# Counts as logarithms in the graph mask, the second graph weights split inside the first attention, and routing operations in another order

## The reference, cut to what matters

```python
def gat_conv(x, edge_index, W, a_src, a_dst, bias, heads, out_ch, concat):
    xl = (x @ W).reshape(n, heads, out_ch)
    alpha_src = einsum('nhc,hc->nh', xl, a_src)
    alpha_dst = einsum('nhc,hc->nh', xl, a_dst)
    e = leaky_relu(alpha_src[src] + alpha_dst[dst], 0.2)
    m = segment_max(e, dst)
    e = exp(e - m[dst])
    s = segment_sum(e, dst)
    alpha = e / (s[dst] + 1e-16)
    out = segment_sum(xl[src] * alpha[:, :, None], dst)
...
h = gat_conv(x, ..., W1, HEADS=4, concat=True)
h1 = relu(layer_norm(h, g1, be1)) + (x @ Wr1 + br1)
h = layer_norm(gat_conv(h1, ..., W2, heads=1), g2, be2) + (h1 @ Wr2 + br2)
...
gate_logits = h2 @ Wg                      # 625 x 8, the best expert of each token
hid = relu(h2 @ W1[expert] + b1[expert])   # 768 -> 3072
y = hid @ W2[expert] + b2[expert]          # 3072 -> 768
```

## Time and profile before

| | |
|---|---|
| median of 3 runs | 1123.75 us (1120.61 to 1124.71) |
| the profiled execution, its own time | 1123.52 us |
| its span in the profile | 1121.6 us |
| PE busy | 1042.5 us (93% of the span) |
| DVE / ACT / POOL busy | 741.3 / 564.8 / 157.0 us |
| mean granted clock of TensorE | 0.974 of full speed |
| transfers | 155.60 MB, mean 139 GB/s |

### The profile page before, as it was taken

How to read it: one execution, slowest core, us unless ns; L and a number is a source line. 1 busy time by engine, 2 the same in 40 slices (tenths; PEclk the granted TensorE clock), 3 DMA queues, 4 the chain that set the end, 5 groups by cost and what they waited for, 6 DMA issues and landing times.

```text
span 1121.6 us, 19089 instructions
## 1 busy us (share of the span) xinstructions
PE 1042.5 (93%) x6181; PEld 651.5 (58%) x6182; DVE 741.3 (66%) x1334; ACT 564.8 (50%) x754; POOL 157.0 (14%) x175
## 2 busy tenths in 40 slices
PE   5999889997999999989989499999999999999997
PEld 3555557764775775556767345555555555555554
DVE  6667767786547764269976698931119898989511
ACT  2667755530451343168843477721118787777311
POOL 2000000040003531054001201100102020302000
PEclk9999999998999999989999599999999999999999
DMA  8300030004507400030014599950007999999200
GB/s 306 104 0 0 1 113 1 1 1 154 126 1 153 81 6 1 1 109 3 2 61 128 214 388 322 390 214 14 24 0 284 386 362 371 373 363 387 84 17 3
DMA packets 92263, 155.60 MB, mean 139 GB/s; under 512 B 36507, under 2 KB 36587, under 8 KB 92214
## 3 DMA queue, kind: packets, MB, share of 16 engines
q1 hardware_dynamic: 89814, 149.20, 38.5%
q0 software_dynamic: 2400, 5.77, 1.4%
HBM read 153.21 MB, written 7.77 MB: 144 GB/s over the span
## 4 chain that ended last, share of the span: by engine, by line
PE 74%; DVE 13%; issue 5%; DMA 3%; ACT 3%; POOL 1%; DVEq 1%; SPq 0%; ACTq 0%; POOLq 0%
PE psum L1493 31%; PE psum L1742 17%; PE psum L1717 16%; DMA low<-in_L_ffn_W_dram 2%; DVE area L1355 2%; PE psum L1481 2%; PE psum L1531 2%; PE psum L1726 2%; DVE smalls L999 1%; PE psum L1632 1%; DVE area L1326 1%; PE psum L1713 1%; DVE area L1086 1%; ACT area L889 1%; ACT low L896 1%
## 5 line engine op out<-in xcount | busy, mean ns | idle before, releaser
L1493 PE MATMUL psum<-area,low 128*125 128x512 f16 (+4 forms) x1116 | 249.3, 384 | 9.9 <-DVE low L1197 6.0
L1355 DVE TENSOR_TENSOR area<-low,area 128x1536 f16<-128x1536 f32 x144 | 246.0, 1754 | 13.4 <-ACT area L948 13.2
L1717 PE MATMUL psum<-area,low 128*128 128x512 f16 x972 | 220.3, 381 | 0.0
L1742 PE MATMUL psum<-area,low 128*128 128x384 f16 x1296 | 219.3, 328 | 0.0
L948 ACT ACTIVATE area<-low 128x1536 f16<-128x1536 f32 x138 | 200.3, 1484 | 37.6 <-DMA low<-in_L_ffn_W_dram 28.8
L1493 PEld LDWEIGHTS psum<-area,low 128*125 128x125 f16 (+2 forms) x1116 | 144.2, 142 | 105.7 <-issue 59.9
L1493 PE MATMUL psum<-area 125*128 125x64 f16 (+10 forms) x1452 | 195.6, 289 | 9.0 <-DVE area L1326 6.0
L1742 PEld LDWEIGHTS psum<-area,low 128*128 128x128 f16 x1296 | 127.0, 98 | 80.9 <-issue 1.7
L1493 PEld LDWEIGHTS psum<-area 125*128 125x128 f16 (+3 forms) x1452 | 126.8, 122 | 60.8 <-DVE area L1326 12.4
L1717 PEld LDWEIGHTS psum<-area,low 128*128 128x128 f16 x972 | 95.2, 98 | 113.7 <-issue 2.5
L959 ACT ACTIVATE low<-psum 128x512 f32<-128x512 f32 x54 | 31.9, 591 | 158.7 <-PE psum L1717 155.7
(11 more groups left out here) (235 smaller groups left out, 1147.8 us busy)
## 6 DMA issues: line engine op xcount, KB each, us to landing
low<-in_L_ffn_W_dram SPq DMA_DIRECT2D x144, 768.0 KB, 8.2
area<-in_L_gnn_W_dram SPq DMA_DIRECT2D x2, 3072.0 KB, 12.0
area<-in_L_gnn_Wr_dram SPq DMA_DIRECT2D x2, 3072.0 KB, 15.6
low<-in_x_dram SPq DMA_DIRECT2D x10, 336.0 KB
area<-in_L_ffn_Wv_dram SPq DMA_DIRECT2D x6, 384.0 KB, 6.3
area<-in_L_ffn_Wq_dram SPq DMA_DIRECT2D x6, 384.0 KB, 6.9
area<-in_L_ffn_Wk_dram SPq DMA_DIRECT2D x6, 384.0 KB, 6.1
area<-in_L_ffn_Wp_dram SPq DMA_DIRECT2D x2, 1152.0 KB, 6.8
```

Of the source, the lines that this page charges most:

```text
L1355: dve.tensor_tensor(low_, raw_view(u), high_, ALU.subtract).then_inc(low_ok, 1)
L1493: ins = pe.matmul(place(name)[0:parts, at:at + w], left(q), right(q)[:, at:at + w], start=(q == 0), stop=(q == k - 1))
L1717: ins = pe.matmul(psum[:, (c % 2) * BANK:(c % 2 + 1) * BANK], ht[x_][:, k, :], w1_s[c][w_][:, k, :], start=False, stop=(k == KD - 1 and x_ ...
L1742: ins = pe.matmul(psum[:, (4 + q) * BANK:(4 + q) * BANK + D // 2], hidT[c % 2][x_][:, j, :], w2_s[c][w_][:, j, q * D // 2:(q + 1) * D // 2 ...
```

## The change

1. **Counts as logarithms.** POOL raises the counts to at least 1, ACT takes their logarithm in place (`logs`), POOL subtracts it from `absent`. DVE's L1126 so adds the mask and the logarithm at once. ACT's Exp gives the row's sum itself (`accum_out`), DVE only adds 1e-16 to it, and PE turns the matrix straight after Exp.
2. **W2 split inside the first attention.** `graph_high` and `graph_low` of W2 are done in two halves of 3072 columns, ACT's at steps 7 and 11, DVE's one step later. `RES1_HALVES` goes from steps 8, 15, 17, 19 to 8, 13, 15, 18. Wr2 is loaded when the second half is done. Behind the attention, `h1T_low(0)` goes ahead of the last join.
3. **Routing.** `ids_first` comes right behind the number of blocks; the table and `routed` come ahead of the places of the tokens; five pairs of small operations for the places become three larger ones; `tokens_low(0)` goes ahead of DVE's wait for `routed`.

```diff
-RES1_HALVES = {8: (1, 0), 15: (1, 1), 17: (2, 0), 19: (2, 1)}
+SPLIT_AT = (7, 11)
+RES1_HALVES = {8: (1, 0), 13: (1, 1), 15: (2, 0), 18: (2, 1)}
...
@@ SP
-            sp.wait_ge(g_low, 1)
+            sp.wait_ge(g_low, 2)
             sp.dma_start(v3(staged, KH), g_Wr2.rearrange("(k p) n -> p k n", p=128)).then_inc(wr2g_in, 16)
...
@@ POOL, ahead of the norms of the first attention
+            for d in range(T):
+                pool.wait_ge(absent_ok, d + 1)
+                pool.tensor_scalar(counts[:, d, :], counts[:, d, :], 1.0, None, ALU.max).then_inc(clamped, 1)
+            for d in range(T):
+                pool.wait_ge(logs_ok, 1 if d < T - 1 else 2)
+                pool.tensor_tensor(absent[:, d, :], absent[:, d, :], counts[:, d, :], ALU.subtract).then_inc(mask_ok, 1)
...
@@ ACT, behind the counting
+            def logs(d0, d1):
+                act.wait_ge(clamped, d1)
+                act.activation(counts[:, d0:d1, :], counts[:, d0:d1, :], ACT.Ln).then_inc(logs_ok, 1)
+
+            logs(0, T - 1)
             no_edge(T - 1)
+            logs(T - 1, T)
...
@@ ACT, attention
                     if 1 <= i <= n:
                         act.wait_ge(neg_ok, g)
-                        act.activation(zbuf[(g - 1) % 4], zbuf[(g - 1) % 4], ACT.Exp, scale=-1.0,
-                                       bias=negm[:, (g - 1) % 4:(g - 1) % 4 + 1]).then_inc(exp_ok, 1)
+                        q = slice((g - 1) % 4, (g - 1) % 4 + 1)
+                        act.activation(zbuf[(g - 1) % 4], zbuf[(g - 1) % 4], ACT.Exp, scale=-1.0, bias=negm[:, q],
+                                       accum_out=rsum[:, q]).then_inc(exp_ok, 1)
...
+                    if layer == 1 and i in SPLIT_AT:
+                        q = SPLIT_AT.index(i)
+                        graph_high(w2g_in, w2_parts, slice(q * KH * D // 2, (q + 1) * KH * D // 2))
...
@@ DVE, attention
+                        if g < T:
+                            dve.wait_ge(mask_ok, i + 1)
                         dve.tensor_tensor_reduce(z, z, absent[:, i % T, :], 1.0, 3e38, ALU.add, ALU.min,
                                                  negm[:, g % 4:g % 4 + 1]).then_inc(neg_ok, 1)
...
                         dve.wait_ge(exp_ok, g)
-                        dve.tensor_tensor_reduce(z, z, counts[:, t, :], 1.0, 1e-16, ALU.mult, ALU.add,
-                                                 rsum[:, q]).then_inc(prob_ok, 1)
+                        dve.tensor_scalar(rsum[:, q], rsum[:, q], 1e-16, None, ALU.add).then_inc(sum_ok, 1)
...
+                    if layer == 1 and i - 1 in SPLIT_AT:
+                        q = SPLIT_AT.index(i - 1)
+                        graph_low(q + 1, w2_parts, slice(q * KH * D // 2, (q + 1) * KH * D // 2))
...
-            dve.wait_ge(absent_ok, T)
...
@@ DVE, between the attentions
             for t in range(3):
                 residual_row(t)
-            graph_low(1, w2_parts)
             for t in range(3):
                 join_residual(t)
-            for t in range(3, T):
-                residual_row(t)
-                join_residual(t)
-            for t in range(3):
+            residual_row(3)
+            join_residual(3)
+            residual_row(4)
+            h1T_low(0)
+            join_residual(4)
+            for t in (1, 2):
                 h1T_low(t)
-            graph_low(2, wr2_parts)
+            graph_low(3, wr2_parts)
...
@@ DVE, routing: behind nblk
+            done(dve, ("ids0",))
+            emptied_by(("ids0",), dve.tensor_scalar(ids_first, place(("ids0",), 1), float(NOWHERE), None, ALU.add))
+            was_emptied(dve, ("ids0",))
+            dve.sem_inc(ids0_ok, 1)
             link(dve.tensor_scalar(active, nblk, 0.0, None, ALU.is_gt))
...
             dve.tensor_copy(nblocks, nblk_sum[0:1, E - 1:E]).then_inc(routed, 1)
+            dve.sem_inc(hid_relu, 2)
+            link(dve.tensor_scalar(base8, start, float(BR), None, ALU.mult))
+            link(dve.tensor_tensor(cum[:, 0:T, :], cum[:, 0:T, :], spread(base8, (P, T, E), 2), ALU.add))
+            link(dve.tensor_tensor(sel, sel, cum[:, 0:T, :], ALU.mult))
+            link(dve.tensor_reduce(pos_f, sel, AX_X, ALU.add))
...
+            dve.tensor_copy(ids_all[:, 1:NB + 1], ids_f).then_inc(ids_ok, 1)
+            tokens_low(0)
             dve.wait_ge(routed, 1)
-            dve.sem_inc(hid_relu, 2)
...
@@ PE
-                        pe.wait_ge(prob_ok, before_ + i)
+                        pe.wait_ge(exp_ok, before_ + i)
```

More of the change, by code:

```diff
@@ L778, in xl2_copy, with graph_high @@
                 emptied_by(("xl2", t), act.activation(xl2[:, t, :], place(("xl2", t), D, P), ACT.Copy, scale=1.0 / SCALE_UP))
-            def graph_high(loaded, high_low):
+            def graph_high(loaded, high_low, columns=slice(0, KH * D)):
                 act.wait_ge(loaded, 16)
-                act.activation(high_low[0], staged, ACT.Copy, scale=SCALE_UP).then_inc(g_high, 1)
+                act.activation(high_low[0][:, columns], staged[:, columns], ACT.Copy, scale=SCALE_UP).then_inc(g_high, 1)
             def weights_high(loaded, whole, high_low):
@@ L1113, in weights_low, with graph_low @@
                                          op1=ALU.subtract).then_inc(w_low, 1)
+            def graph_low(n, high_low, columns=slice(0, KH * D)):
+                dve.wait_ge(g_high, n)
+                dve.scalar_tensor_tensor(out=high_low[1][:, columns], in0=staged[:, columns], scalar=SCALE_UP,
+                                         in1=high_low[0][:, columns], op0=ALU.mult, op1=ALU.subtract).then_inc(g_low, 1)
             def graph_attention(layer, heads, width, agg, bias_row, behind=None):
@@ L1173, in _ @@
             shifted1(T - 1).then_inc(epi_b, 1)
-            def graph_low(n, high_low):
-                dve.wait_ge(g_high, n)
-                dve.scalar_tensor_tensor(out=high_low[1], in0=staged, scalar=SCALE_UP, in1=high_low[0], op0=ALU.mult,
-                                         op1=ALU.subtract).then_inc(g_low, 1)
             def residual_row(t):
@@ L1370, in _, with tokens_low @@
             was_emptied(dve, ("gate", T - 1))
+            def tokens_low(b):
+                dve.wait_ge(hthi_ok, b + 1)
+                dve.tensor_tensor(ht[1], turned, ht[0], ALU.subtract).then_inc(ht_ok, 1)
             def by_token(ap, n=E):
@@ L1398, in _ @@
             link(dve.tensor_tensor(order, active_sum, active, ALU.subtract))
-            link(dve.tensor_scalar(base8, start, float(BR), None, ALU.mult))
-            done(dve, ("ids0",))
-            ins = dve.tensor_scalar(ids_first, place(("ids0",), 1), float(NOWHERE), None, ALU.add)
-            emptied_by(("ids0",), ins)
-            was_emptied(dve, ("ids0",))
-            dve.sem_inc(ids0_ok, 1)
-            for t in range(T):
-                link(dve.tensor_tensor(cum[:, t, :], cum[:, t, :], base8, ALU.add))
-                link(dve.tensor_tensor_reduce(junk8, cum[:, t, :], sel[:, t, :], 1.0, 0.0, ALU.mult, ALU.add,
-                                              pos_f[:, t:t + 1]))
-            link(dve.tensor_tensor(reached, by_token(pos_f, NB + 1), spread(first_rows, (P, T, NB + 1), 2), ALU.is_ge))
-            link(dve.tensor_reduce(block_of, reached[:, :, 1:NB + 1], AX_X, ALU.add))
-            link(dve.scalar_tensor_tensor(out=row_in, in0=block_of, scalar=float(-BR), in1=pos_f, op0=ALU.mult, op1=ALU.add))
-            for t in range(T):
-                dve.tensor_scalar(row_hot[:, t, :], iota128, row_in[:, t:t + 1], None, ALU.is_equal)
-            link(dve.tensor_tensor(here, reached[:, :, 0:NB], reached[:, :, 1:NB + 1], ALU.subtract))
-            dve.tensor_tensor(here16, here, by_token(token_id, NB), ALU.mult).then_inc(spots_ok, 1)
             def over(ap, keep):
@@ L1422, in _ @@
             link(dve.tensor_tensor(match, match, prod, ALU.mult))
-            done(dve, ("ids",))
-            emptied_by(("ids",), dve.tensor_scalar(ids_f, place(("ids",), NB), float(NOWHERE), None, ALU.add))
-            was_emptied(dve, ("ids",))
-            dve.tensor_copy(ids_all[:, 1:NB + 1], ids_f).then_inc(ids_ok, 1)
             for q, what in enumerate((iota8, order)):
@@ L1436, in _ @@
             dve.tensor_copy(nblocks, nblk_sum[0:1, E - 1:E]).then_inc(routed, 1)
+            dve.sem_inc(hid_relu, 2)
[3 more added lines that the diff above has]
+            link(dve.tensor_reduce(pos_f, sel, AX_X, ALU.add))
+            link(dve.tensor_tensor(reached, by_token(pos_f, NB + 1), spread(first_rows, (P, T, NB + 1), 2), ALU.is_ge))
+            link(dve.tensor_reduce(block_of, reached[:, :, 1:NB + 1], AX_X, ALU.add))
+            link(dve.scalar_tensor_tensor(out=row_in, in0=block_of, scalar=float(-BR), in1=pos_f, op0=ALU.mult, op1=ALU.add))
+            for t in range(T):
+                dve.tensor_scalar(row_hot[:, t, :], iota128, row_in[:, t:t + 1], None, ALU.is_equal)
+            link(dve.tensor_tensor(here, reached[:, :, 0:NB], reached[:, :, 1:NB + 1], ALU.subtract))
```

(12 more changed lines are left out.)

15 lines of the change are left out of this document (7 added, 8 removed).

## The result

The changed kernel takes 1111.99 us (median of 5 runs, 1110.96 to 1117.14); the kernel before, run beside it, 1121.01 us (median of 5). The ratio is 0.992, 95% interval 0.9903 to 0.9937: 9.0 us less, against 9.2 forecast. In a later series, beside 23 runs of the kernel before (1120.91 us), it took 1110.57, a ratio of 0.9898 (0.9878 to 0.9918). The ratios leave disturbed executions out and are not exactly the quotient of the two medians (in the later series that would be 0.9908). So the total came as forecast. The steps did not all: this profile and twelve runs show that two errors in the first attention cancelled each other, and that the routing gained its part in another way.

The account below looks back on a forecast made before the run. PE, busy 93% of the span, was taken as the bound, so only its waits or lower clock could be won. 5.1 between the attentions, 2.7 clock and 1.4 routing made 9.2 us less: about 1114 us, range 1108 to 1119.

Parts of the forecast that it names:

- The start: Start of the first attention: POOL's subtractions and DVE's operations take turns, first agg at 161.3 instead of 157.6, 3.7 us lost.
- rival B: Start of the first attention: POOL does not hold DVE up, first agg 4.6 us earlier, total 1110 us; chance 0.24.
- 3 x 1.5: Start of the first attention: three POOL subtractions of 1.5 us each fall between DVE's first four operations.
- the chain from 139.9 us: Mask preparation from ACT's first free moment: source row copied at 148.8 instead of 148.1, DVE's first pair 150.3 instead of 149.6.
- rival E: Routing and clock give nothing: transfers set the pace, or the start's wait lowers the clock; 1116 us, chance 0.12.
- L1134 taken out: First attention: PE's last four waits for DVE's multiplication by the counts go, 4.8 us gained.
- The splits: W2's halves on ACT and DVE inside the first attention: 1.0 us exposed, bounds 0 and 12 us.
- Rival C: First attention: W2's splits are exposed, 11 us more there, total 1125 us, no difference; chance 0.13.
- The attention's end: PE's end of the first attention: 241.2 + 3.7 - 4.8 + 1.0 = 241.1 us, rounded down to 240.8.
- Between the attentions: From the first attention to xl2(0): start at 264.7 instead of 269.8, 5.1 us; clock holds, another 2.7 us.
- The routing: Routing before the experts: rows 1.24 us earlier, third unit's split 1.35 us earlier; 1.4 us taken, ends 0 and 2.2.
- D: First attention: ACT reloads activation tables with every unit, 42 us slower, total about 1156 us; chance 0.03.

Follow-up runs that it names:

- logarithms alone: Only the counts as logarithms (point 1 of the change) put into the kernel before: 1118.27 us, ratio 0.9965.
- rows first: Changed kernel, but SP holds weight unit 5, with 6 and 7 behind it, until the first block's rows have landed: 1116.68 us, ratio 0.994.
- DVE's masks: Changed kernel, but idle DVE does the last maximum and all five subtractions instead of POOL: 1107.20 us, ratio 0.9859; run again 1104.82 us, ratio 0.9853.
- the split alone: Only the split of W2 inside the first attention (point 2 of the change) put into the kernel before: 1116.86 us, ratio 0.9956.

## Why the prediction was right, and where it was not

- **The start.** The mechanism was right (POOL and DVE work in turns, and rival B is false), its size was too large. The second Exp was to come 5.9 us later, made up of 0.7 for a later first pair, 0.7 for the rest of a subtraction and "3 x 1.5". It came 3.75 us later, counted from the source row's turns, and PE's two waits for Exp came to 3.6 us where 5 or more were named. The first 0.7 is a slip: the terms of the chain from 139.9 us add up to 148.2 and not to 148.8, and DVE had its first pair when it had it before (3.08 us behind the turns, 3.07 before). The second 0.7 was 0.1. The 1.5 us of one subtraction was right (1.52), but three of DVE's operations were stretched by only 1.2 us each. From the source row's turns to the first agg it was 12.55 us instead of 11.01, so 1.5 us were lost and not 3.7. But the step stopped there: the wait that it foresaw took the clock down, which cost another 1.65 us (logarithms alone) to 3.2 us (this trace). I had named this only as a part of rival E; together the start cost 3.2 to 4.7 us. Rival B's price was wrong too: with POOL out of the way the first agg comes 9.01 us behind the turns, a gain of 2.0 us and not 0.9.
- **L1134 taken out.** The forecast was 4.8 us, and 6.06 were measured. The term left out what PE loses after each wait, some 0.3 us apiece.
- **The splits.** The forecast was 1.0 us; 1.1 to 1.2 were measured. The attention takes 92.87 us with them (rows first) and 91.78 without (logarithms alone) at nearly the same lapse, and its part behind the second head's source row takes 76.60 with them (DVE's masks) and 75.38 without. In the trace two waits of 0.45 and 0.16 us stand at steps 7 and 11. Rival C is out. Without the logarithms the splits cost 3.2 us.
- **The attention's end** was forecast for 240.8 and came at 240.76. That is luck: +3.7 - 4.8 + 1.0 = -0.1 stood for about +4.7 - 6.1 + 1.2 = -0.2.
- **Between the attentions.** The forecast was a start of xl2(0) at 264.7 us and 7.8 us for it; measured were 264.80 and 8.01. PE's wait is 1.56 us for 1.5, and row 4's copy and `h1T_low` are last in the chain, as said. This carried the result: 4.57 us of the way from the attention's end to xl2(0), and 2.5 us of clock.
- **The routing.** The forecast was 1.35 us; about 1.2 are shown in the traces, by another way, and that they agree is luck again. The step said that the rows "land, are turned and have their high part 1.24 us earlier". They landed 0.3 us earlier on the mean of three traces each, since the weight transfers ahead set their landing. What remains is the 0.94 us behind `routed` that `tokens_low` no longer waits for. The step had this too, but took 0.7 us of register loads off again, between `tokens_low` and the third split; they do not show there, since L1376 starts 0.88 us after L1394, as L1355 started 0.87 after L1449.
- **Rivals D and E.** There were two table loads of 1.28 us, no more, and both lay under waits (ACT still waits 0.81 us for POOL after the first and 0.99 for DVE after the second), so D is out. The Trainium skill ("ScalarE: Activation LUTs", table sets) names a set that holds both functions; this program, as compiled, loads twice. Of E, the lapse at the start came true, but both the routing and the clock at xl2(0) gave their part.

What the sum did not hold at all is how single executions differ; the cause of that is not known. From the third split to the end, which the change does not touch, the traces need 480.2 to 485.1 us. PE's 30 turns between 553 and 569 us take either 3.59 or 5.09 us, and this trace has the longer case. So its span is only 6.7 us shorter than before, where the medians differ by 9.0.

## What to carry over

Work for POOL that fits into its idle time is not free if DVE has operations with two SBUF inputs at that moment, as it had here: give it to an idle DVE, or end it before. A wait of PE costs more than its length once the clock lapses behind it (3.25 us of waiting here cost up to 3.2 more), so look at what the first matmuls behind a wait take. Before moving an operation forward, find out what its transfer will queue behind.

## What was not expected of the hardware

- The clock lapses behind a wait that is little longer than those it survives: two waits of 1.44 and 1.50 us two microseconds apart leave it at 1.00, and one of 1.76 us (the split alone) is followed by a product of 3.93 us instead of 2.32. Behind the same wait of 3.25 us the lapse is not always as long: the first agg takes 3.94 to 4.63 us, and the granted clock from 157 to 166 us is 0.62 in one trace and 0.81 in another (logarithms alone).
- A subtraction of 125x625 takes some 0.7 us on DVE and 1.5 on POOL. When POOL subtracts while DVE does operations of the same size with two inputs, each of either takes 2.0 to 2.1 us.
- A fetch of 128 rows by index, issued while weight transfers run at 390 GB/s, needed up to 6.44 us; with the transfers held back, 2.93.
